# A pipelined cross-attention kernel: projections four tiles ahead of the scores in place of five

## The chip, the cores and the metric

The kernel runs on one core of a Trainium2 chip. The metric is the device time of one execution in microseconds (us); lower is better. Three runs of the kernel before took 222.98, 226.28 and 222.8 us, median 222.98. The core's compute engines are TensorE (PE), VectorE (DVE), ScalarE (ACT) and GpSimd (POOL); SyncE (SP) issues nearly all transfers. Each engine works through its own instructions in order, and they meet at semaphores.

## What is computed

Three residual blocks follow one another on 64 tokens of width 256: a cross attention to a context of 6272 rows, a self attention with 16 heads on dequantised weights, and a gated mixture of experts. The change touches the first, cut here to its core:

```python
q = x @ Wq.T;  k_raw = context @ Wk.T;  v_raw = context @ Wv.T     # 32 heads of 8
kv = concatenate([k_raw, v_raw], -1).reshape(b, m, 32, 8, 2);  k, v = kv[..., 0], kv[..., 1]
q = _rmsnorm(q);  k = _rmsnorm(k)              # over the 8 of a head
scores = einsum('bhnd,bhmd->bhnm', q, k) * 8 ** -0.5
out = einsum('bhnm,bhmd->bhnd', softmax(scores, -1), v)
x = x + out;  x = x + self_attention(layernorm(x));  x = x + experts(layernorm(x))
```

## The kernel before, in words

The context is cut into T = 49 tiles of 128 rows. Every engine walks the same sequence of steps t = FIRST .. LAST, written by `steps` (L94): warm-up steps with negative t, a hardware loop whose body holds eight steps, and closing steps. In one step an engine does its part for several tiles, each at its own distance from t. The constants of L55 are these distances: PROJ = 5, KV = 4, TR = 3, PV = -1. `step` of each engine asks for `t.ahead(distance)` and leaves the part out where that tile does not exist.

The way of tile k through a step pipeline:

- SP loads its context into `ctx_f` (four slots), `load`, L265.
- DVE rounds it to `ctx_hi` (`split_context`, L539, step k-PROJ-1) and POOL makes the rest `ctx_lo` (L351, same step). Both have two slots.
- PE projects keys and values into one of two PSUM banks: six matmuls of 512 columns, L809, L812 and L815, at the end of step k-PROJ.
- The keys' chain, step k-KV: ACT squares (`k_sq`, L421), DVE sums each head (`k_ss`, L557) and copies the values (L566), ACT takes logarithm and exponent (`k_ln` L431, `k_r` L435), DVE scales (`k_n`, L575) and writes the first two float16 parts of the keys (L583). For the first KV tiles (`HEAD = KV`) ACT copies the values, L424.
- POOL writes the third part (L357, semaphore `k2_done`), step k-TR.
- SP turns the keys with a DMA transpose, `k` to `kT`, both with four slots (`turn`, L272, L278). It waits for `k2_done` of its tile.
- PE multiplies queries and turned keys: the scores, two halves of eight matmuls, L773, step k. It waits for the turned keys (L767). ACT exponentiates each half (`exps`, L409) into `room`; the first half stands ahead of that step's `k_sq` in ACT's order, the second behind it.
- PE multiplies with the values one step later (L787).

So in PE's step t come the scores of tile t, the values of tile t-1, and the projection of tile t+PROJ.

SP's order is written apart from the steps: in `for t in range(2, T + LAG)` (L304, LAG = 7) it turns tile t-7, then loads context t, and on every third round issues codes (512 KB, one piece of the self attention's weights) or the scales for them. In this order: turn of a tile k that is a multiple of 3, load, codes; turn k+1, load, scales; turn k+2, load. The load waits for `ctx_lo` of tile t-4. POOL multiplies codes by scales (`dequantise`, L334, L343) at the end of its steps t = 3, 6, 9, ..., 48. The queries' own path (`queries_mm`, `queries_copied`, `queries_squared`, `queries_rms`, `queries_split`, `queries_turned`, `queries_placed`) is hung into the warm-up steps by the dictionaries at L437, L601 and L818.

In short, a "turn" below is one DMA transpose of SP, and S(k) is the moment at which the scores of tile k begin on PE.

Of the kernel before, what the change touches and what calls it, by code (L numbers as in the profile page):

```python
# [51 lines left out]
HC = H // 2  # L52
NR = E // 2 + 1
U = 8
PROJ, KV, TR, PV = 5, 4, 3, -1  # L55
FIRST, LAST = -(PROJ + 1), T - PV
HEAD = KV
LOOP0 = 1 - PV
# [35 lines left out]
def steps(engine, body, after):  # L94


    for c in range(FIRST, LOOP0):
        body(Tile(None, c))
        if c in after:
            after[c]()  # L100
    with engine.Fori(0, ITERS) as i:
        for j in range(U):
            body(Tile(i, LOOP0 + j))
    for c in range(LOOP1, LAST + 1):
        body(Tile(None, c))
# [8 lines left out]
def perceiver(nc, x, ctx_t, xwq, xwkv, codes, scales, wo_scales, qkv_bias, bo, gate_w, gate_bias,  # L114
              up_w, down_w, eye, expert_ids, pair_heads, out):
    with ExitStack() as stack:
# [256 lines left out]
        def _(act):  # L373
# [60 lines left out]
                    wait(act, kn_done, r.count(plus=-1))  # L434
                    nc.scalar.activation(k_r[:, a], k_ln[:, a], ACT.Exp, scale=-0.5).then_inc(r_done, 1)  # L435

            steps(act, step, {-4: queries_copied, -3: queries_rms})  # L437

            layernorm_act(act, "ln2")

# [54 lines left out]
        def _(dve):  # L495
# [102 lines left out]
                        values_copied(r)  # L598
                        keys_scaled(r)

            steps(dve, step, {-4: queries_squared, -3: queries_split, -2: queries_placed})  # L601


            dve.wait_ge(pv_done, 2 * T)
# [114 lines left out]
        def _(pe):  # L719
# [95 lines left out]
                        last = nc.tensor.matmul(ps_kv[a], ctx_lo[:, a, c], wkv_hi[:, c], start=False, stop=(c == DC - 1))  # L815
                    last.then_inc(kv_mm, 1)

            steps(pe, step, {-5: queries_mm, -2: queries_turned})  # L818

            pe.wait_ge(ready("o_sb"), 1)  # L820
            for h in range(2):
# [207 lines left out]
```

## Time and profile before

| | kernel before |
|---|---|
| median of three runs | 222.98 us |
| the profiled execution, its own time | 221.69 us |
| its span | 219.9 us |
| PE busy | 203.6 us, 93% |
| ACT busy | 147.5 us, 67% |
| DVE busy | 129.9 us, 59% |
| POOL busy | 106.8 us, 49% |
| granted TensorE clock, mean | 0.995 |
| transfers | 39.63 MB, mean 180 GB/s |

The profiled execution has its own time, 221.69 us, beside the median of the runs; its span, first to last instruction, is 1.8 us shorter. A PE busy for 93% need not be PE at its peak, and the share is an average over stages: the warm-up to 19.4 us, 49 tiles of cross attention to about 171 us, and then the self attention and the experts, which the change does not touch.

### The profile page before, as it was taken

The page shows a single profiled execution, that of the slowest core. Times are in us where ns is not written, and L with a number is a line of the kernel's source. Part 1 is how long each engine was busy: PE and PEld are TensorE (multiplying, and loading weights), DVE is VectorE, ACT ScalarE, POOL GpSimd, SP SyncE. Part 2 cuts the span into 40 slices and gives each one's busy share as a digit, 9 for nine tenths or more (in the row PEclk, how much of TensorE's full clock was granted, in tenths as well). Part 3 has the DMA queues.
Part 4 walks back from the last instruction along what each step waited for, and adds up shares of the span by engine and source line. Part 5 has one row for each costly group of instructions (what it writes and reads, how often), then busy time and mean ns, then how long its engine had stood idle before and what let it go on. Part 6 is the DMA issues. An engine that isn't in the chain of part 4 may idle for free.

```text
span 219.9 us, 7814 instructions
## 1 busy us (share of the span) xinstructions
PE 203.6 (93%) x2973; PEld 135.4 (62%) x2973; DVE 129.9 (59%) x325; ACT 147.5 (67%) x285; POOL 106.8 (49%) x125
## 2 busy tenths in 40 slices
PE   7676899999999999999999999999878889988993
PEld 2354577777777777777777777777656424463441
DVE  1688548666676776758676675776730522835721
ACT  3456788888888888888888888988789013313230
POOL 4335647748576665867658576665737000000000
PEclk9999999999999999999999999999999999999998
DMA  5429999999889998988979999999999997000000
GB/s 184 122 70 226 174 253 216 149 241 247 222 223 202 208 194 205 227 216 213 198 198 202 221 220 200 255 183 234 147 278 248 289 287 211 28 3 0 0 3 12
DMA packets 66816, 39.63 MB, mean 180 GB/s; under 512 B 54007, under 2 KB 60599, under 8 KB 66799
## 3 DMA queue, kind: packets, MB, share of 16 engines
q1 hardware_dynamic: 66367, 38.95, 79.1%
q10 hardware_dynamic: 432, 0.46, 0.7%
q8 instruction: 10, 0.16, 0.3%
q14 instruction: 7, 0.06, 0.1%
HBM read 26.49 MB, written 0.07 MB: 121 GB/s over the span
## 4 chain that ended last, share of the span: by engine, by line
PE 79%; DMA 7%; DVE 6%; ACT 3%; issue 2%; POOL 2%; ACTq 0%; DVEq 0%
PE ps L787 20%; PE ps L809 13%; PE ps L773 11%; PE ps L815 9%; PE ps L812 9%; PE ps L837 5%; DMA kT<-k 5%; PE ps L927 3%; DMA ctx_f<-ctx_t 2%; PE ps L943 2%; PE ps L888 2%; PE ps L846 1%; PE ps L876 1%; POOL k L357 1%; PE ps L935 1%
## 5 line engine op out<-in xcount | busy, mean ns | idle before, releaser
L409 ACT ACTIVATE room<-ps 128x1024 f32<-128x1024 f32 x98 | 100.2, 1029 | 21.1 <-PE ps L773 21.0
L351 POOL TENSOR_TENSOR ctx_lo<-ctx_f,ctx_hi 128x256 fp32r<-128x256 f32 x49 | 36.0, 734 | 54.6 <-DVE ctx_hi L551 52.2
L787 PE MATMUL ps<-room,v_flat 128*17 128x128 f32 x1568 | 52.3, 274 | 0.0
L809 PE MATMUL ps<-wkv_hi,ctx_hi 128*128 128x512 f32 x98 | 43.7, 446 | 2.6 <-DVE k_n L575 1.5
L787 PEld LDWEIGHTS ps<-room,v_flat 128*17 128x17 f32 x1568 | 38.6, 97 | 5.3 <-ACT room L409 0.3
L583 DVE CAST k<-k_n 128x512 f16<-128x512 f32 x49 | 37.9, 774 | 2.6
L812 PE MATMUL ps<-wkv_lo,ctx_hi 128*128 128x512 f32 x98 | 38.8, 396 | 0.4 <-DVE wkv_lo L502 0.4
L343 POOL TENSOR_TENSOR w_all<-w_all,s_ring 128x1024 f32<-128x1024 f32 x16 | 37.9, 2375 | 0.0
L575 DVE TENSOR_TENSOR k_n<-ps,k_r 128x256 f32<-128x256 f32 x49 | 20.8, 424 | 25.2 <-ACT k_r L435 25.2
L357 POOL TENSOR_TENSOR k<-k_n,k 128x256 f16<-128x256 f32 x49 | 33.1, 675 | 5.0 <-DVE k L583 5.0
L773 PEld LDWEIGHTS ps<-q_blk,kT 48*128 48x128 f16 x784 | 22.1, 94 | 21.7 <-issue 13.5
L773 PE MATMUL ps<-q_blk,kT 48*128 48x128 f16 x784 | 31.0, 218 | 3.5 <-DMA kT<-k 1.9
L557 DVE TENSOR_REDUCE k_ss<-k_sq 128x32 f32<-128x256 f32 x49 | 20.3, 415 | 21.9 <-ACT k_sq L421 21.9
L815 PE MATMUL ps<-wkv_hi,ctx_lo 128*128 128x512 f32 x98 | 30.8, 395 | 0.0
L809 PEld LDWEIGHTS ps<-wkv_hi,ctx_hi 128*128 128x128 f32 x98 | 18.4, 187 | 15.0 <-issue 8.6
L815 PEld LDWEIGHTS ps<-wkv_hi,ctx_lo 128*128 128x128 f32 x98 | 18.4, 188 | 4.3
L812 PEld LDWEIGHTS ps<-wkv_lo,ctx_hi 128*128 128x128 f32 x98 | 18.5, 189 | 2.8 <-DVE wkv_lo L502 0.7
L421 ACT ACTIVATE k_sq<-ps 128x256 f32<-128x256 f32 x49 | 18.5, 378 | 2.4 <-PE ps L815 2.4
L431 ACT ACTIVATE k_ln<-k_ss,eps_rms 128x32 f32<-128x32 f32 x49 | 16.1, 328 | 4.5 <-DVE k_ss L557 4.3
L566 DVE COPY v_flat<-ps 128x256 f32<-128x256 f32 x45 | 18.5, 412 | 0.0
L551 DVE CAST ctx_hi<-ctx_f 128x256 fp32r<-128x256 f32 x48 | 13.6, 283 | 0.1
L435 ACT ACTIVATE k_r<-k_ln 128x32 f32<-128x32 f32 x49 | 11.3, 230 | 1.6
(113 smaller groups left out, 123.0 us busy)
## 6 DMA issues: line engine op xcount, KB each, us to landing
w_all<-codes SPq DMA_DIRECT2D x16, 512.0 KB, 4.2
ctx_f<-ctx_t SPq DMA_DIRECT2D x48, 128.0 KB, 2.8
up_sb<-up_w SPq DMA_DIRECT2D x5, 704.0 KB, 10.1
s_ring<-scales SPq DMA_DIRECT2D x12, 256.0 KB, 3.8
s_ring<-wo_scales SPq DMA_DIRECT2D x4, 512.0 KB, 5.4
dn_sb<-down_w SPq DMA_DIRECT2D x5, 352.0 KB
kT<-k SPq DMA_TRANSPOSE x49, 3.7
wkv_f<-xwkv ACTq DMA_DIRECT2D x1, 256.0 KB, 3.2
```

What stands on the lines that cost most here:

```text
L343: nc.gpsimd.tensor_tensor(w, w, s, ALU.mult).then_inc(ring_free[u % RING], 1)
L351: nc.gpsimd.tensor_tensor(ctx_lo[:, split.slot(2)], ctx_f[:, split.slot(4)], ctx_hi[:, split.slot(2)].bitcast(F32), ALU.subtract).then_inc ...
L357: nc.gpsimd.tensor_tensor(key_part(keys, 2), k_n[:, keys.slot(2)].rearrange("p (r h d) -> p r h d", h=2, d=XD), key_part(keys, 0), ALU.sub ...
L409: nc.scalar.activation(probs[:, t.slot(2), half], ps_scores[half].rearrange("p b n -> p (b n)"), ACT.Exp).then_inc(exp_done, 1)
L557: nc.vector.tensor_reduce(k_ss[:, r.slot(2)], k_sq[:, r.slot(2)].rearrange("p (h d) -> p h d", d=XD), AX_X, ALU.add).then_inc(ss_done, 1)
L575: nc.vector.tensor_tensor(kn, ps_kv[r.slot(2)][:, 0:D].rearrange("p (h d) -> p h d", d=XD), k_r[:, r.slot(2)].unsqueeze(2).to_broadcast([P ...
L583: nc.vector.tensor_copy(key_parts(r)[:, :, :, 0:2, :], pairs.unsqueeze(3).to_broadcast([P, PAIRS, 2, 2, XD])).then_inc(k1_done, 1)
L773: last = nc.tensor.matmul(ps_scores[half][:, e, at:at + P], kT[rows, t.slot(4), r // 2], q_blk[rows, r // 2].rearrange("p h n -> p (h n)") ...
L787: last = nc.tensor.matmul(ps_o[CT * j:CT * j + VW, g * P:(g + 1) * P], v_sb[:, t.slot(8), r], probs[:, t.slot(2), half, at:at + P], start= ...
L809: nc.tensor.matmul(ps_kv[a], ctx_hi[:, a, c], wkv_hi[:, c], start=(c == 0), stop=False)
L812: nc.tensor.matmul(ps_kv[a], ctx_hi[:, a, c], wkv_lo[:, c], start=False, stop=False)
L815: last = nc.tensor.matmul(ps_kv[a], ctx_lo[:, a, c], wkv_hi[:, c], start=False, stop=(c == DC - 1))
```

## The change

The three distances ahead of the scores are each one smaller, the distance of the values stays, and the queries' steps move by one, so that they still stand behind the same projections. `FIRST`, `HEAD` and the loop's bounds follow from the constants.

```diff
-PROJ, KV, TR, PV = 5, 4, 3, -1
+PROJ, KV, TR, PV = 4, 3, 2, -1
...
-            steps(act, step, {-4: queries_copied, -3: queries_rms})
+            steps(act, step, {-3: queries_copied, -2: queries_rms})
...
-            steps(dve, step, {-4: queries_squared, -3: queries_split, -2: queries_placed})
+            steps(dve, step, {-3: queries_squared, -2: queries_split, -1: queries_placed})
...
-            steps(pe, step, {-5: queries_mm, -2: queries_turned})
+            steps(pe, step, {-4: queries_mm, -1: queries_turned})
```

On PE, at the end of the warm-up, this is the difference of the orders; L756 turns the queries, L773 is the first tile's scores, the rows of L809, L812 and L815 are one projection.

```order
 L815 MATMUL ps<-wkv_hi,ctx_lo 128x512 x2
 L756 MATMUL ps<-ident,q_room 128x64 x8
-L809 MATMUL ps<-wkv_hi,ctx_hi 128x512
-L812 MATMUL ps<-wkv_lo,ctx_hi 128x512
-L809 MATMUL ps<-wkv_hi,ctx_hi 128x512
-L812 MATMUL ps<-wkv_lo,ctx_hi 128x512
-L815 MATMUL ps<-wkv_hi,ctx_lo 128x512 x2
 L773 MATMUL ps<-q_blk,kT 128x128 x16
```

The projection of tile 4 no longer stands ahead of the scores of tile 0; it comes behind them, and every later projection stands behind one more tile's scores and values.

On ACT at the same place, L421 to L435 are the keys' chain and L409 is an exponent. Before:

```order
L421 ACTIVATE k_sq<-ps 128x256
L424 ACTIVATE v_flat<-ps 128x16x16
L431 ACTIVATE k_ln<-k_ss,eps_rms 128x32
L435 ACTIVATE k_r<-k_ln 128x32
L421 ACTIVATE k_sq<-ps 128x256
L424 ACTIVATE v_flat<-ps 128x16x16
L431 ACTIVATE k_ln<-k_ss,eps_rms 128x32
L435 ACTIVATE k_r<-k_ln 128x32
L409 ACTIVATE room<-ps 128x1024
L421 ACTIVATE k_sq<-ps 128x256
L409 ACTIVATE room<-ps 128x1024
```

The change:

```order
L421 ACTIVATE k_sq<-ps 128x256
L424 ACTIVATE v_flat<-ps 128x16x16
L431 ACTIVATE k_ln<-k_ss,eps_rms 128x32
L435 ACTIVATE k_r<-k_ln 128x32
L409 ACTIVATE room<-ps 128x1024
L421 ACTIVATE k_sq<-ps 128x256
L409 ACTIVATE room<-ps 128x1024
```

These are tiles 2, 3 and 4 before, and tiles 2 and 3 now: the chain of tile 3 has come behind the first exponent of tile 0.

On POOL, L351 makes `ctx_lo` and L357 the third part of the keys; the first dequantisation (L343) stands some rows below the piece.

```order
 L351 ISA
 L351 TENSOR_TENSOR ctx_lo<-ctx_f,ctx_hi 128x256 x4
-L357 TENSOR_TENSOR k<-k_n,k 128x16x2x8
-L351 TENSOR_TENSOR ctx_lo<-ctx_f,ctx_hi 128x256
 L357 TENSOR_TENSOR k<-k_n,k 128x16x2x8
 L351 TENSOR_TENSOR ctx_lo<-ctx_f,ctx_hi 128x256
```

One pair less stands ahead of each dequantisation. Before, the keys that come behind it are those of tiles 7, 10, 13, ...; now they are those of tiles 6, 9, 12, .... SP's order is the same in both kernels.

## Rows read from the trace of the kernel before

**Rows 1.** The table by stretches; columns named in its first row.

```profile
core 0: us, PE busy (x) PEld busy (x) DVE busy (x) ACT busy (x) POOL busy (x), PEclk, DMA share, GB/s
32.82:155.48 122.66, 122.66 (x2107) 89.18 (x2107) 84.04 (x195) 104.24 (x196) 83.79 (x92) 1.00 0.98 213
```

**Rows 2.** Timeline, PE: start us, us, operation; scores of tiles 1, 2, 4, 43, 44, 47.

```profile
22.43 0.62 PE L773 MATMUL ps<-q_blk,kT 48*128 48x128 f16 x16
...
26.53 0.62 PE L773 MATMUL ps<-q_blk,kT 48*128 48x128 f16 x16 [0.89 <-DMA kT<-k]
...
32.82 0.62 PE L773 MATMUL ps<-q_blk,kT 48*128 48x128 f16 x16
...
155.48 0.62 PE L773 MATMUL ps<-q_blk,kT 48*128 48x128 f16 x16
...
159.48 0.62 PE L773 MATMUL ps<-q_blk,kT 48*128 48x128 f16 x16 [0.79 <-DMA kT<-k]
...
166.11 0.62 PE L773 MATMUL ps<-q_blk,kT 48*128 48x128 f16 x16 [0.23 <-DMA kT<-k]
```

**Rows 3.** Timeline, all engines: the chain of tile 31, from S(27) to its turn.

```profile
105.16 0.62 PE L773 MATMUL ps<-q_blk,kT 48*128 48x128 f16 x16
...
106.60 0.38 ACT L421 ACTIVATE k_sq<-ps 128x256 f32<-128x256 f32 x1
...
107.82 2.37 POOL L343 TENSOR_TENSOR w_all<-w_all,s_ring 128x1024 f32<-128x1024 f32 x1
...
108.85 1.61 DVE L583 CAST k<-k_n 128x512 f16<-128x512 f32 x1
...
111.45 0.67 POOL L357 TENSOR_TENSOR k<-k_n,k 128x256 f16<-128x256 f32 x1
...
112.14 1.23 SPq L278 DMA_TRANSPOSE kT<-k  x1
```

**Rows 4.** Timeline, SP's queue: turns of tiles 30 and 32, codes, scales.

```profile
107.89 1.26 SPq L278 DMA_TRANSPOSE kT<-k  x1
...
109.82 0.42 SPq L281 DMA_DIRECT2D w_all<-codes  x1
...
114.05 0.57 SPq L287 DMA_DIRECT2D s_ring<-scales  x1
114.71 1.26 SPq L278 DMA_TRANSPOSE kT<-k  x1
```

**Rows 5.** L278 alone: issue to landing of the turns of tiles 30, 31, 32.

```profile
DMA to landing us min/median/max: 2.8/2.8/2.8
...
DMA to landing us min/median/max: 2.7/2.7/2.7
...
DMA to landing us min/median/max: 3.8/3.8/3.8
```

**Rows 6.** Timeline, SP's queue: first codes behind tile 3, turns of tiles 4, 5.

```profile
25.77 0.43 SPq L281 DMA_DIRECT2D w_all<-codes  x1
26.30 1.24 SPq L278 DMA_TRANSPOSE kT<-k  x1
...
28.88 1.62 SPq L278 DMA_TRANSPOSE kT<-k  x1
```

**Rows 7.** L278 alone: issue to landing of the turns of tiles 4 and 5.

```profile
DMA to landing us min/median/max: 5.1/5.1/5.1
...
DMA to landing us min/median/max: 6.9/6.9/6.9
```

**Rows 8.** L278 alone, by stretch: 50 to 132 us, 132 to 161 us.

```profile
DMA to landing us min/median/max: 2.7/3.2/4.4
...
DMA to landing us min/median/max: 3.1/4.7/7.7
```

**Rows 9.** The chain that ended last, in order of time: start us, us, what.

```profile
18.46 0.86 DVE q_blk L536 x2
...
160.29 5.77 DMA kT<-k
```

## The prediction

> **What bounds the kernel now.** I read first the table by stretches, then PE's timeline. Between S(4) and S(43) PE is busy for all of its 122.66 us, at a granted clock of 1.00 [rows 1]; the two starts lie 39 tiles apart [rows 2], so a step takes (155.48 - 32.82) / 39 = 3.145 us. ACT, the next engine, has 104.24 us of work there, 2.67 us a step, DVE and POOL 84 us, 2.15 us a step [rows 1]. So PE sets the step, and no other engine's amount of work is near it. Then I looked at what PE waits for outside this stretch. S(2), S(44) and S(47) each end a wait for turned keys, of 0.89, 0.79 and 0.23 us [rows 2]. The keys arrive just in time there. The question is how early they arrive in between.
>
> For that I followed one tile. Tile 31's chain begins on ACT behind the first exponent of step 27. S(27) is 105.16, its square starts at 106.60, the third part of the keys on POOL at 111.45, the turn is issued at 112.14 [rows 3] and lands 2.7 us later [rows 5], at 114.84. S(31) is 32.82 + 27 x 3.145 = 117.74. The keys lie ready for 2.9 us. The same for its neighbours: tile 30 is issued at 107.89 [rows 4] and lands 2.8 us later [rows 5], 3.9 us ahead of S(30) = 114.59; tile 32 is issued at 114.71 [rows 4], lands 3.8 us later [rows 5], 2.4 us ahead of S(32) = 120.88. This pattern of three comes from the weights: the dequantisation of 2.37 us [rows 3] stands ahead of tile 31's keys on POOL, and the scales are issued 0.66 us ahead of tile 32's turn [rows 4].
>
> **What the change does.** It adds no instruction and takes none away. The chain of a tile starts where it did relative to its projection, but the scores come one step, 3.145 us, sooner behind it. So each slack above shrinks by 3.145 us: 3.9 becomes +0.8, 2.9 becomes -0.2, 2.4 becomes -0.7. What had been cover is gone.
>
> PE is in order, so a wait for keys holds the next projection too, and with it the chain of a later tile. The first exponent of step t waits for the scores of t, and the square behind it on ACT is now that of tile t+3. So there is a closed loop: S(t) to landed keys of t+3 to S(t+3), with three steps, 9.44 us, to run in where there were four, 12.58. Where the loop takes longer, PE waits. The sum goes by stretches.
>
> *Middle, tiles 12 to 37.* The dequantisation moves to the tiles that are multiples of 3, and SP's order does not. Such a tile is turned S + 6.98 (112.14 - 105.16, [rows 3]), then come a load, the codes, and at once the next tile's turn. Codes follow a turn by 109.82 - 107.89 = 1.93 us [rows 4]. Today 2.3 us pass from codes to the next turn; with the late turn ahead of them about 0.5 us are left. One turn of today stands like that: tile 4's, 0.53 us behind its codes [rows 6]. It took 5.1 us [rows 7], landing 5.6 us behind the codes' issue. So the keys of tile 3n+1 land 6.98 + 1.93 + 5.3 to 5.6 = 14.2 to 14.5 us behind S(3n-3), and have four steps, 12.58 us. The excess of 1.6 to 1.9 us is met by two waits, three tiles apart, since the four steps hold a waiting step at either end: 0.8 to 0.95 us for each three tiles. If the codes delayed nothing, the multiples of 3 would still need 6.98 + 2.8 = 9.78 us, 0.34 over 9.44. Nine groups of three give 3.1 to 8.6 us. I take 0.8 each, 7.2 us, because the crowded turn is the nearer row.
>
> *Start, tiles 0 to 11.* Tile 4's projection no longer runs ahead of S(0), but S(0) waits for the placed queries, 18.46 plus 0.86 us [rows 9], as before: nothing gained. S(2) stays near 26.5. Tile 5's turn was issued 28.88 - 22.43 = 6.45 us after S(1) [rows 2, 6] and took 6.9 us [rows 7]. After S(2) the same chain ends at 26.53 + 6.45 + 6.9 = 39.9; S(5) was 35.97. That is +3.9 us, or +2.1 with tile 4's 5.1 us. The next tile of its kind, 8, may lose the lower of the two once more. Ends 2.1 and 6.0; I take 3.5, as a slower pace also unloads the queue.
>
> *Late, tiles 38 to 46.* The turns from 132 us on take 4.7 us in the median and up to 7.7, against 3.2 before that [rows 8]; now the scales are 512 KB each and stand ahead of the turns of tiles 38, 41, 44. Tile 32, of this kind, is turned S(28) + 6.4 (114.71 - 108.30, [rows 4]; S(28) from the step), so with 4.7 us tiles 38 and 41 need 11.1 us, 1.7 over 9.44 each. Tile 44 needed 159.4 - S(40) = 159.4 - 146.0 = 13.4 us, since S(44) waited for it [rows 2]: 4.0 over. Together 7.4; at least the 0.34 of above each, 1 us. I take 4 us, about half.
>
> *End.* S(44) to S(47) is 6.63 us [rows 2]. Tile 47's square now stands behind S(44), not S(43). From S(43) = 155.48 to its turn at 160.29 are 4.8 us [rows 2, 9], and the landing takes 5.8. So S(47) is 10.6 us behind S(44): +4.0 us; with a landing of 2.8 us +1.0. I take 2.5. One step less runs without a projection, where exponents bound; that gain (rival 3) is swallowed by this wait.
>
> Sum: 221.69 + 7.2 + 3.5 + 4 + 2.5 = 238.9 us for the profiled execution. The median of the runs stands 1.3 us above that execution, so 240 us. The ends of the four terms are 2.1 + 3.1 + 1 + 1 = 7 us and 26 us, that is 230 and 249.
>
> Beside this, the Trainium skill, "DMA: Bandwidth & Descriptors", Queues, rings and completion order, says that each engine consumes the descriptors of a ring in ring order, so what SP issues later waits behind its codes; the 5.1 us of a turn 0.53 us behind codes [rows 6, 7] agrees. The same page, Latency and other measured facts, says that lighter HBM load makes the fixed part of a transfer smaller; that speaks for rival 1.
>
> **Rivals.**
>
> 1. *The landings shrink.* With the DMA engines at 0.98 [rows 1], a slower pace may give the turns back their short landing, 2.8 us [rows 5], everywhere. For: the same instruction takes 2.7 to 7.7 us. Against: the crowding behind codes is a matter of order, and gets worse. Then the middle and late stretches cost 0.34 us per three tiles, 12 times, 4 us, the end 1 and the start 1: 228 to 230 us. Chance 0.2.
>
> 2. *Everything adds.* All recorded landings stay, and the late turns push one another: 6.0 + 8.6 + 7.4 + 4 = 26 us on top, 248 to 249 us and a little beyond, since a late tile can find its queue fuller still. Chance 0.13.
>
> 3. *No slower.* POOL and SP catch up because the chain, not PE, is what waits. What is left is the gain of one step less without a projection: such steps are bound by two exponents of about 1.0 us and PE's order around them, some 2.4 us against PE's 1.6, so 0.8 us. This needs every loop within 9.44 us, and decides at the point where tile 32's kind falls from 3.145 x 4 - 2.4 = 10.2 us by 0.7. For: nothing in the rows. 222 us. Chance 0.03.
>
> 4. *The clock falls.* The waits would take PE to its half clock; the other rivals are at 2.4 GHz, the granted 1.00. Against: the wait of 0.89 us ahead of S(2) [rows 2] left it there. If it happened for a tenth of the tiles, 5 tiles x 3 us, 15 more: 255 us. Chance 0.02.
>
> **How the numbers follow.** My forecast has 0.62, and its own range is 232 to 247. To hold 8 in 10, the range takes in most of rival 1 and reaches to the edge of rival 2: 229 to 249. A difference of 2%, 4.5 us, is about what a measurement of this kernel can tell from no change: slower by more means above 227.4. Only the lowest part of rival 1 and rival 3 lie below. Faster by over 2% has no source in the rows: 0.01. Within 2%: 0.05. Slower: 0.94.
>
> **What would show it.** In the changed kernel's trace PE waits for the turned keys, with L773 released by the DMA to `kT` or by the turn's issue, 10 to 17 us in all, where the trace of before has three, 1.9 us together [rows 2]. The step is 3.4 us on average, in a pattern of three: one wait of 0.8 us or more at tiles 3n+1, none or little at the others, and the turn of 3n+1 takes about 5 us with codes issued some 0.5 us ahead. ACT, DVE and POOL busy times stay as they are. From S(44) to S(47) more than 8 us pass. Self attention and experts take the same time as before. The prediction is wrong if the step stays below 3.2 us (then landings shrank), if the waiting tiles are of another kind (then I misjudged the loop), or if the start, to S(5), costs nothing.

## The result, and the profile after

| | before | changed |
|---|---|---|
| median | 222.89 us (4 runs) | 243.08 us (239.25 to 244.4, 4 runs) |
| ratio to before | | 1.083, 95% interval 1.063 to 1.104 |
| span of the profiled execution | 219.9 us | 241.0 us |
| PE busy | 203.6 us | 209.5 us, the same 2973 matmuls |
| granted TensorE clock, mean | 0.995 | 0.97 |

The change makes the kernel 8% slower. The ratio is taken over the runs outside the chip's slower state, 242.79 and 239.25 us for the changed kernel, so it is smaller than that of the medians. The forecast was 240 us, its range 229 to 249.

The table by stretches for the changed kernel, S(12) to S(37), where the kernel before needs 78.63 us:

```profile
core 0: us, PE busy (x) PEld busy (x) DVE busy (x) ACT busy (x) POOL busy (x), PEclk, DMA share, GB/s
62.49:151.87 89.38, 80.87 (x1351) 58.20 (x1351) 54.93 (x127) 66.37 (x126) 54.89 (x59) 0.98 0.82 189
```

PE is no longer busy throughout [rows 1]; 8.5 us are idle, and the rest is busy for longer at a clock of 0.98. No other engine has become the bound: ACT's share fell, and so did that of the DMA engines, from 0.98 to 0.82. What took over is latency. The waits of the changed kernel (engine, line waited for; us in total, times, longest us):

```profile
PE ps L773 <- DMA kT<-k: 17.0, 17, 3.1
PEld ps L773 <- DMA kT<-k: 6.4, 5, 3.4
```

The kernel before had three such waits of 1.9 us [rows 2]. (The weight loads of PE wait beside its matmuls; the two are not added.) The page's chain that ended last:

```profile
PE 38%; DMA 22%; issue 12%; ACT 8%; DVE 8%; POOL 6%; SPq 3%; ACTq 0%; DVEq 0%; POOLq 0%
```

Before, PE held 79% of that chain and DMA 7%. Now a turn of the keys stands in it, and ahead of it ACT, DVE and POOL, one after the other: the loop itself is the path. PE's timeline over two of its pieces, S(34) to S(41):

```profile
140.80 0.62 PE L773 MATMUL ps<-q_blk,kT 48*128 48x128 f16 x16
143.95 0.62 PE L773 MATMUL ps<-q_blk,kT 48*128 48x128 f16 x16
147.37 0.62 PE L773 MATMUL ps<-q_blk,kT 48*128 48x128 f16 x16 [0.21 <-DMA kT<-k]
151.87 0.62 PE L773 MATMUL ps<-q_blk,kT 48*128 48x128 f16 x16 [1.29 <-DMA kT<-k]
155.32 0.62 PE L773 MATMUL ps<-q_blk,kT 48*128 48x128 f16 x16 [0.23 <-DMA kT<-k]
158.47 0.62 PE L773 MATMUL ps<-q_blk,kT 48*128 48x128 f16 x16
161.61 0.62 PE L773 MATMUL ps<-q_blk,kT 48*128 48x128 f16 x16
165.39 0.62 PE L773 MATMUL ps<-q_blk,kT 48*128 48x128 f16 x16 [0.57 <-DMA kT<-k]
```

Steps without a wait are still 3.15 us. The long wait stands at tile 37, a tile 3n+1. SP's queue ahead of it, and the landing of that turn:

```profile
144.50 1.25 SPq L278 DMA_TRANSPOSE kT<-k  x1
...
146.42 0.42 SPq L281 DMA_DIRECT2D w_all<-codes  x1
146.94 1.23 SPq L278 DMA_TRANSPOSE kT<-k  x1
...
DMA to landing us min/median/max: 4.8/4.8/4.8
```

Tile 36, the multiple of 3, is turned 6.84 us after S(33) = 137.66; codes follow 1.92 us later; tile 37's turn is 0.52 us behind them and lands in 4.8 us, at 151.75, 5.3 us behind the codes. S(37) is 151.87. Before, the same kind of turn landed in 2.7 us [rows 3, 5].

By stretches, from the starts of the scores on PE in both traces (us; changed minus before is what the span lost):

| | before | changed | lost |
|---|---|---|---|
| start to S(0) | 19.41 | 20.46 | 1.05 |
| S(0) to S(12) | 38.57 | 42.03 | 3.5 |
| S(12) to S(37) | 78.63 | 89.38 | 10.75 |
| S(37) to S(44) | 22.87 | 23.80 | 0.9 |
| S(44) to S(48) | 8.24 | 12.83 | 4.6 |
| S(48) to the end | 52.2 | 52.5 | 0.3 |

The stretch from S(44) on holds one projection more than before: the step from S(44) to S(45) now projects tile 48 and takes 3.16 us, where it took 1.61.

### The profile page after: what moved, and what is told of

Same layout as the page of the kernel before. It is cut to its first block, busy times and chain, and to the rows that moved or that the text cites. A ratio compares the mean times of both kernels' runs of the same rounds, so it can differ in the third digit from the quotient of the medians.

```text
span 241.0 us, 7820 instructions
## 1 busy us (share of the span) xinstructions
PE 209.5 (87%) x2973; PEld 138.5 (57%) x2973; DVE 130.7 (54%) x326; ACT 146.9 (61%) x284; POOL 108.0 (45%) x125
## 4 chain that ended last, share of the span: by engine, by line
PE 38%; DMA 22%; issue 12%; ACT 8%; DVE 8%; POOL 6%; SPq 3%; ACTq 0%; DVEq 0%; POOLq 0%
DMA kT<-k 21%; PE ps L787 6%; PE ps L773 5%; PE ps L837 5%; PE ps L809 4%; PE ps L815 3%; POOL k L357 3%; PE ps L812 3%; ACT room L409 3%; POOL ctx_lo L351 3%; PE ps L927 3%; DVE k_n L575 2%; PE ps L943 2%; ACT k_sq L421 2%; ACT k_ln L431 2%
## 5 line engine op out<-in xcount | busy, mean ns | idle before, releaser
L409 ACT ACTIVATE room<-ps 128x1024 f32<-128x1024 f32 x98 | 100.5, 1029 | 43.4 <-PE ps L773 43.4
L351 POOL TENSOR_TENSOR ctx_lo<-ctx_f,ctx_hi 128x256 fp32r<-128x256 f32 x49 | 37.3, 761 | 71.5 <-DVE ctx_hi L551 69.9
L787 PE MATMUL ps<-room,v_flat 128*17 128x128 f32 x1568 | 53.6, 278 | 0.3 <-ACT room L409 0.3
L773 PE MATMUL ps<-q_blk,kT 48*128 48x128 f16 x784 | 31.7, 223 | 19.8 <-DMA kT<-k 17.0
L773 PEld LDWEIGHTS ps<-q_blk,kT 48*128 48x128 f16 x784 | 23.1, 97 | 39.1 <-issue 26.5
L809 PE MATMUL ps<-wkv_hi,ctx_hi 128*128 128x512 f32 x98 | 44.6, 455 | 0.7 <-DVE k_n L575 0.7
L787 PEld LDWEIGHTS ps<-room,v_flat 128*17 128x17 f32 x1568 | 39.1, 98 | 6.3 <-ACT room L409 0.7
L812 PE MATMUL ps<-wkv_lo,ctx_hi 128*128 128x512 f32 x98 | 39.6, 404 | 0.0
L343 POOL TENSOR_TENSOR w_all<-w_all,s_ring 128x1024 f32<-128x1024 f32 x16 | 37.8, 2363 | 1.2 <-DMA s_ring<-wo_scales 1.2
L583 DVE CAST k<-k_n 128x512 f16<-128x512 f32 x49 | 37.0, 755 | 2.1
L357 POOL TENSOR_TENSOR k<-k_n,k 128x256 f16<-128x256 f32 x49 | 33.1, 676 | 4.1 <-DVE k L583 4.1
L815 PE MATMUL ps<-wkv_hi,ctx_lo 128*128 128x512 f32 x98 | 32.3, 411 | 0.0
L809 PEld LDWEIGHTS ps<-wkv_hi,ctx_hi 128*128 128x128 f32 x98 | 18.6, 189 | 13.4 <-issue 9.0
L815 PEld LDWEIGHTS ps<-wkv_hi,ctx_lo 128*128 128x128 f32 x98 | 19.1, 196 | 4.8 <-POOL ctx_lo L351 0.3
L421 ACT ACTIVATE k_sq<-ps 128x256 f32<-128x256 f32 x49 | 18.5, 378 | 3.8 <-PE ps L815 3.8
L812 PEld LDWEIGHTS ps<-wkv_lo,ctx_hi 128*128 128x128 f32 x98 | 18.9, 193 | 2.5 <-DVE wkv_lo L502 0.2
L435 ACT ACTIVATE k_r<-k_ln 128x32 f32<-128x32 f32 x49 | 11.3, 230 | 1.6
```

Of the source, the lines that this page charges most:

```text
L343: nc.gpsimd.tensor_tensor(w, w, s, ALU.mult).then_inc(ring_free[u % RING], 1)
L351: nc.gpsimd.tensor_tensor(ctx_lo[:, split.slot(2)], ctx_f[:, split.slot(4)], ctx_hi[:, split.slot(2)].bitcast(F32), ALU.subtract).then_inc ...
L357: nc.gpsimd.tensor_tensor(key_part(keys, 2), k_n[:, keys.slot(2)].rearrange("p (r h d) -> p r h d", h=2, d=XD), key_part(keys, 0), ALU.sub ...
L409: nc.scalar.activation(probs[:, t.slot(2), half], ps_scores[half].rearrange("p b n -> p (b n)"), ACT.Exp).then_inc(exp_done, 1)
L421: nc.scalar.activation(k_sq[:, a], ps_kv[a][:, 0:D], ACT.Square).then_inc(sq_done, 1)
L583: nc.vector.tensor_copy(key_parts(r)[:, :, :, 0:2, :], pairs.unsqueeze(3).to_broadcast([P, PAIRS, 2, 2, XD])).then_inc(k1_done, 1)
```

## The experiments

Theory: the distance sets a loop, S(t) to landed keys of t+3, that has three steps to run in, and its longest member, a turn crowded behind 512 KB of codes, decides. Rivals: the shorter distance costs whatever stands in the queues; the landings are set by the load of the DMA engines and not by order; the clock.

Each run below is the changed kernel with one edit, except where said. "Middle" is S(12) to S(37) in its trace: 78.6 us before, 89.4 us changed. The kernel before had a median of 222.80 us beside four of the runs (TR = 3 alone, little traffic, hardly any dequantisation, dequantisation one step later) and 222.75 us beside the other four.

### A shorter chain: the third part of the keys one step earlier

```diff
-PROJ, KV, TR, PV = 4, 3, 2, -1
+PROJ, KV, TR, PV = 4, 3, 3, -1
```

> The changed kernel with one number different: TR = 3, so POOL makes the third part of the keys one step earlier in its own order, ahead of the next tile's ctx_lo instead of behind it, and the turn can be issued about 1 us earlier (near S + 4.9 us in place of 5.7 to 7.0). Theory (a loop of three steps, S to landed keys, is too long by 0.3 to 1.9 us): every loop now fits in 9.44 us, PE no longer waits in the middle, 221 to 226 us. Rival (the turns' landing behind codes and scales is what costs, whenever they are issued): the waits stay, 233 us or more.

Measured: 239.44 us (238.46 to 239.99), ratio 1.078 (1.071 to 1.085). The middle takes 86.75 us. The number is the rival's; my theory had overlooked something. Most turns do go out 4.8 to 5.0 us after their S, 0.9 us sooner. But tile 37's, 0.52 us behind the codes again, lands in 4.9 us, and the start grows too: S(0) to S(12) takes 44.4 us, 42.03 in the changed kernel. POOL and SP show why:

```profile
140.43 2.44 POOL L343 TENSOR_TENSOR w_all<-w_all,s_ring 128x1024 f32<-128x1024 f32 x1
142.83 0.91 POOL L351 TENSOR_TENSOR ctx_lo<-ctx_f,ctx_hi 128x256 fp32r<-128x256 f32 x1
```

```profile
143.81 0.34 SPq L270 DMA_DIRECT2D ctx_f<-ctx_t  x1
144.20 0.42 SPq L281 DMA_DIRECT2D w_all<-codes  x1
144.72 1.24 SPq L278 DMA_TRANSPOSE kT<-k  x1
```

The load that follows the turn of 3n waits for a `ctx_lo` that stands behind the dequantisation on POOL, as it did before the edit. What the edit moved is the turn: its keys now stand ahead of the dequantisation, so the turn goes out early and the load has to wait. SP is in order, so the codes wait with it and leave just ahead of the next turn. The next run takes this one wait away.

### The same, with the load's wait moved one tile back

```diff
-PROJ, KV, TR, PV = 4, 3, 2, -1
+PROJ, KV, TR, PV = 4, 3, 3, -1
...
-LAG = 7
+LAG = 6
```

With LAG = 6 the load behind the turn of tile k is that of tile k+6 in place of k+7, and waits for the `ctx_lo` of tile k+2 in place of k+3.

> The changed kernel with TR = 3 and LAG = 6. TR = 3 alone left a wait at tiles 3n+1: SP's load behind the turn of 3n waits for a ctx_lo that then stands behind the dequantisation, so load and codes went out 0.5 us ahead of the next turn. With LAG = 6 that load waits for a ctx_lo made before, codes go out 2 us behind the turn of 3n, and 2.3 us stay ahead of the turn of 3n+1. Theory (loop length, with crowding by order as its largest piece): every loop is at most 9.5 us (5.9 + 2.8, 5.3 + 4.2), PE waits in hardly any step of the middle, 221 to 227 us. Rival (three steps of distance are too few whatever stands in the queues, or the load of DMA itself makes the landings): 234 us or more.

Measured: 228.98 us (227.6 to 230.88), against 222.75 us for the kernel before beside it, ratio 1.027 (1.021 to 1.033). That is 2 us above my expectation, and 10.5 us less than the run above, for one load's place. In the two traces 7.8 us of it come in the middle and 5.6 us from S(0) to S(12); S(0) itself is 1.9 us later. SP's queue for the same tiles, and the landing of tile 37's turn:

```profile
130.49 1.25 SPq L278 DMA_TRANSPOSE kT<-k  x1
131.83 0.53 SPq L270 DMA_DIRECT2D ctx_f<-ctx_t  x1
132.41 0.42 SPq L281 DMA_DIRECT2D w_all<-codes  x1
134.45 1.23 SPq L278 DMA_TRANSPOSE kT<-k  x1
...
DMA to landing us min/median/max: 2.9/2.9/2.9
```

2.04 us instead of 0.52 lie between codes and turn, and the turn lands in 2.9 us; over the middle such turns, 1.7 to 2.0 us behind the codes, take 2.9 to 3.8 us. The middle is PE's own again:

```profile
59.34:138.25 78.91, 78.75 (x1352) 57.13 (x1352) 51.80 (x125) 66.30 (x126) 54.71 (x59) 1.00 0.95 209
```

So three steps of distance are enough in the middle, at a DMA share of 0.95, with little to spare: the keys of tiles 28, 29 and 32 land 0.15 us or less ahead of their scores. The crowding of the middle came from the order in SP's queue, not from the load of the DMA engines, which is higher here than in the changed kernel. LAG = 6 without TR = 3 was not run. What is left over the kernel before lies in the start (S(12) is 1.4 us later), at the late tiles 38 and 43 (2.1 us together; tile 38's turn stands 0.69 us behind 512 KB of scales, tile 43's 1.98 us behind codes), and at the end: S(44) to S(48) takes 12.57 us against 8.24.

### Little traffic from codes and scales

The loads of codes and scales bring 64 columns; POOL fills the whole unit from the scales.

```diff
-                sp.dma_start(w_all[:, u], codes[:, u]).then_inc(codes_in[u % RING], 16)
+                sp.dma_start(w_all[:, u, 0:64], codes[:, u, 0:64]).then_inc(codes_in[u % RING], 16)
...
+                w = w_all[:, u].rearrange("p (c n) -> p c n", n=64)
+                s = s_ring[:, u % RING, 0:64].unsqueeze(1).to_broadcast([P, WS // 64, 64])
-                nc.gpsimd.tensor_tensor(w, w, s, ALU.mult).then_inc(ring_free[u % RING], 1)
+                nc.gpsimd.tensor_tensor(w, s, s, ALU.mult).then_inc(ring_free[u % RING], 1)
```

> The changed kernel with codes and scales loaded for 64 columns alone, one eighth to one sixteenth of the bytes; POOL multiplies broadcast scales over the whole unit, so its time stays and the self attention's weights are not the real ones. Theory (ring order behind 512 KB): all turns land in 2.7 to 3 us, the wait at 3n+1 goes, what is left is 6.98 + 2.8 = 9.8 us for the multiples of 3, 0.34 us per three tiles: 224 to 229 us. Rival (the latency is in the engines' chain): 236 us or more.

Measured: 230.38 us (229.62 to 231.13), ratio 1.037 (1.030 to 1.045). Landings and the middle; below them the changed kernel's landings from 62 to 129 us:

```profile
DMA to landing us min/median/max: 2.7/2.7/3.0
...
61.44:140.22 78.78, 78.70 (x1352) 57.13 (x1352) 50.41 (x125) 66.29 (x126) 49.57 (x59) 1.00 0.58 132
```

```profile
DMA to landing us min/median/max: 2.7/3.5/5.6
```

The chain on the engines is as in the changed kernel, and PE does not wait: the loss of the middle is in the landings. Even the 0.34 us per three tiles that I had left for the multiples of 3 is gone; they are turned 6.1 to 6.7 us after their S in place of 6.6 to 7.0, and fit but for one wait of 0.15 us. The total is 1.4 us above the expected interval: in the trace S(0) to S(12) still loses 3.0 us against the kernel before, S(44) to S(48) takes 12.5 us and loses 4.3, and 1.7 us are lost behind S(48).

Codes and scales are hardly the cause of the first two: beside the same small loads the turns of the middle land in 2.7 to 3.0 us, and yet six turns of this trace take 4.2 to 5.2 us, those of tiles 4, 7, 9, 43, 46 and 48; every other from tile 1 on takes at most 3.1. From the DMA queues (packets, MB, share) while tile 48's turn is under way, and that turn's landing; below them the one queue that is used from 75 to 149 us, where no turn takes over 2.9 us:

```profile
q8 instruction: 1, 0.02, 1.7%
...
kT<-k SPq DMA_TRANSPOSE x1, 4.5
```

```profile
q1 hardware_dynamic: 30532, 9.77, 58.2%
```

Each of the six turns has one packet of 16 KB on q8 under way, of the kind that the profile calls `instruction`, for 0.9 to 1.3 us, which ends 2.6 to 3.2 us behind the turn's issue; the turn lands 1.2 to 2.0 us behind that packet's end. No other turn of the trace has such a packet later than 0.7 us behind its issue, and from 51 to 157 us there is none. (Packets of 8 KB of the same kind, on q14 at 64, 74 and 149 us, stand beside turns of 2.7 to 2.8 us.) So a turn can be late beside a load of program code as well as behind codes. That is read off the trace and was not tested by an edit.

### Hardly any dequantisation

POOL multiplies 8 columns of each row by their scales and leaves the others as they were loaded; all loads stay.

```diff
-                nc.gpsimd.tensor_tensor(w, w, s, ALU.mult).then_inc(ring_free[u % RING], 1)
+                part = (slice(None), slice(None), slice(0, 8)) if u < NQKV else (slice(None), slice(0, 8))
+                nc.gpsimd.tensor_tensor(w[part], w[part], s[part], ALU.mult).then_inc(ring_free[u % RING], 1)
```

> The changed kernel with dequantisation on 8 columns per row in place of 512 or 1024, so that it takes far less than 2.37 us on POOL (the self attention's weights are not the real ones); all loads stay. Theory: the multiples of 3 are turned 1.1 us sooner, at S + 5.75, codes leave sooner, and keys 3n+1 land S(3n-3) + 5.75 + 1.93 + 5.4 = 13.1 against 12.6: about 0.25 us per three tiles instead of 0.8 to 1, and the start and the late stretch gain alike: 227 to 233 us. Rival (transfers alone decide): 238 us or more.

Measured: 235.78 us (232.44 to 239.19), too spread for an interval, and between my two numbers. The middle takes 82.35 us, 3.7 over the kernel before, where I expected about 2. The multiples of 3 are turned 5.7 to 6.1 us after their S, the turns of 3n+1 land in 2.7 to 4.7 us. So the dequantisation has a part in the loss by what it does to SP's timing, as the theory says, but less clearly than the transfers.

### Dequantisation one step later

```diff
-DEQ0, DEQ = 3, 3
+DEQ0, DEQ = 4, 3
```

> The changed kernel with dequantisation at POOL's steps 4, 7, 10 in place of 3, 6, 9, which puts it ahead of the keys of tiles 3n+1 again, as in the kernel before, with 2.3 us between codes and that turn. Theory: the crowded turn of 3n+1 (5 us) goes away and the waits of 1.4 us at tiles 3n+1 with it; the next longest loop is that of tiles 3n+2 with 6.3 + 3.9 = 10.2 us, so PE waits there, up to 0.76 us per three tiles: 232 to 238 us. Rival (only the alignment of dequantisation and codes costs, not the shorter distance): within 2 us of the kernel before, 225 us.

Measured: 241.09 us (239.25 to 242.43), ratio 1.088 (1.081 to 1.096): no gain that the intervals separate, 3 us above my expectation. The middle is 83.68 us, 5.7 us better than the changed kernel, and the waits are where I expected them: 0.7 to 0.9 us at tiles 3n+2 (20, 26, 32), about 0.2 at 3n+1. The late tiles lost part of what the middle had won: S(37) to S(44) takes 26.2 us against 23.8, with waits of 1.6, 1.5 and 0.9 us at tiles 38, 43 and 44. The turns of 38 and 44 stand 0.7 and 1.5 us behind scales of 512 KB. In these traces the alignment moves the loss more than it removes it.

### One distance less again

`PROJ, KV, TR = 3, 2, 1`, the queries' steps packed into steps -3 to -1.

```diff
-PROJ, KV, TR, PV = 4, 3, 2, -1
+PROJ, KV, TR, PV = 3, 2, 1, -1
...
-LOOP0 = 1 - PV
+LOOP0 = 3 - PV
```

> Distances one smaller again: PROJ, KV, TR = 3, 2, 1, the queries' steps packed into the warm-up steps -3 to -1. Theory (the step is the loop from S to landed keys over PROJ - 1 steps): loops of 8.5 to 9.8 us over two steps, 4.2 to 4.9 us a step in place of 3.4, that is 280 to 305 us. Rival (each distance less costs a fixed wait as this change did, 18 to 21 us): 258 to 266 us.

Measured: 289.5 us, one run.

```profile
73.68:182.34 108.66, 80.41 (x1351) 57.25 (x1352) 45.60 (x126) 66.28 (x125) 55.13 (x59) 1.00 0.60 154
```

A step is 108.66 / 25 = 4.35 us, so a loop of two steps is 8.7 us, 5.7 to 6 us to the turn and 2.8 for the landing: the queue is slack (share 0.60) and the bare loop is what is seen. A loop of 8.7 us fits into three steps of PE, 9.44, and not into two, 6.29. One run of 289.5 us is far outside the rival's 258 to 266.

### The clock over the first scores

```diff
                 last.then_inc(ready("qT_mm"), 1)
+                for _ in range(11):
+                    nc.tensor.matmul(ps[:, 7, :], zeros[:, 0:P], zeros[:], start=True, stop=True, skip_group_check=True)
```

> The changed kernel with eleven extra matmuls on zeros (128 x 512, float16, about 2.4 us) behind the turned queries, into a free PSUM bank, where PE waits 2.6 us for the placed queries. Theory: the granted clock stays up over the first scores, tile 4's projection takes 1.6 instead of 2.3 us, S(1) and S(2) come up to 1 us sooner, and the middle does not change: 0 to 2 us less than the changed kernel. Rival (the clock is no part of the loss): the projection takes 2.3 us as before.

In the changed kernel PE waits 2.62 us for the placed queries, where the kernel before projects tile 4, and works at half clock after it (L815 takes 1.05 in place of 0.63 us):

```profile
20.46 0.62 PE L773 MATMUL ps<-q_blk,kT 48*128 48x128 f16 x16 [2.62 <-DVE q_blk L536]
...
22.36 1.05 PE L815 MATMUL ps<-wkv_hi,ctx_lo 128*128 128x512 f32 x2
```

With the filler, in the trace of its slowest run (248.82 us):

```profile
18.26 2.55 PE L760 MATMUL ps<-zeros 128*128 128x512 f16 x11
20.95 0.62 PE L775 MATMUL ps<-q_blk,kT 48*128 48x128 f16 x16
...
22.53 0.63 PE L817 MATMUL ps<-wkv_hi,ctx_lo 128*128 128x512 f32 x2
24.06 0.62 PE L775 MATMUL ps<-q_blk,kT 48*128 48x128 f16 x16 [0.90 <-DMA kT<-k]
```

The projection runs at full clock, and a wait of 0.90 us for tile 1's keys spends what it wins. S(2) still comes 0.55 us sooner behind S(0) than in the changed kernel; at S(4), which waits 2.6 us for keys, nothing is left (15.2 us from S(0), 14.2 in the changed kernel). Measured: 244.61 us (242.96 to 248.82), ratio 1.096 (1.088 to 1.103): no gain. The clock does fall at this place in the changed kernel, and keeping it up here brought nothing that the runs can tell; the falls elsewhere were not tested.

### The two numbers of TR = 3 and LAG = 6 on the kernel before

TR is one more and LAG one less here too.

```diff
-PROJ, KV, TR, PV = 5, 4, 3, -1
+PROJ, KV, TR, PV = 5, 4, 4, -1
...
-LAG = 7
+LAG = 6
```

> The kernel before, distances 5, 4 and the keys' third part and SP's order as in the run above: TR = 4, LAG = 6. Theory: the step is PE's own 3.145 us already, so 1 us more slack for each tile gains nothing in the middle, and only the three waits of 1.9 us at tiles 2, 44 and 47 can go: 219 to 223 us. Rival (waits hidden in the rows cost PE time in the middle of the kernel before): 217 us or less.

Measured: 220.74 us (219.77 to 222.98, 12 runs) against 222.75 us (17 runs), ratio 0.9913 (0.9876 to 0.9949): 0.9% faster, small but clear of 1, and the fastest of the versions here. The middle is 78.6 us as before, S(2) and S(44) wait for no keys, one wait of 0.55 us is left at S(47), and the keys lie ready 2.8 to 4.9 us ahead of the scores in the middle. Its S(0) was at 20.74 in this trace, 1.3 us later than in the kernel before, and S(2) was at 26.53 all the same. The spans differ by only 0.6 us in the two profiled executions; that the other 1.4 us of the medians come from such late starts, which more slack absorbs, is a guess that no run here tests.

## Why the prediction was right or wrong

- **What bounds, and what takes over**: right. PE's 3.145 us a step stayed where no wait stood, and PE came to wait for turned keys, 17.0 us in 17 waits, at the top of the 10 to 17 us given.
- **Middle, 7.2 us forecast, 10.75 measured.** From S(19) to S(37) 5.3 us are lost in 18 tiles, 0.88 us for each three; the sum had 0.8, its reason 0.8 to 0.95. The parts of the loop measured 6.84 + 1.92 + 5.3 us at tile 37, forecast 6.98 + 1.93 + 5.3 to 5.6. I spread the excess over two waits, and it came as one of about 1.3 to 1.5 us at every second tile 3n+1 (19, 25, 31, 37) with 0.2 to 0.3 us around it. The mis-sized term is tiles 12 to 19, with 5.5 us lost: tile 13 alone waited 2.14 us, its turn taking 5.6 us and landing 6.4 us behind the codes where the sum had at most 5.6; and behind that wait came the clock.
- **The clock**, rival 4 with 0.02: it happened, in small. Behind the wait at tile 13 the projection's first matmul takes 0.79 us for 0.50, and the next step is 4.41 us long:

```profile
67.85 0.62 PE L773 MATMUL ps<-q_blk,kT 48*128 48x128 f16 x16 [2.14 <-DMA kT<-k]
68.40 1.07 PE L787 MATMUL ps<-room,v_flat 128*17 128x128 f32 x32
69.40 0.79 PE L809 MATMUL ps<-wkv_hi,ctx_hi 128*128 128x512 f32 x1
```

  That is 1.3 us, and 0.3 in the step after it, of half clock (1.2 GHz); the waits of 1.3 us at tiles 19 to 37 left it up. Over the whole kernel PE is busy 5.9 us longer for the same matmuls. The prediction had argued from one wait of 0.89 us; the late and closing terms of my own sum held waits of more than 2 us. How much of the 5.9 us lies on the path is not settled; near S(0) the filler gained nothing.
- **Start, 3.5 us forecast, 1.05 + 3.5 measured.** Size about right, place half wrong: tile 5 waits for nothing, its turn landing in 4.1 us and not 6.9; tiles 4 (1.1 us), 7 (2.2) and 10 (0.5) wait, which are 3n+1 as in the middle. But the crowding of the middle does not explain them: the codes were issued 1.0 to 2.3 us ahead, not 0.5, and with little traffic the same stretch still loses 3.0 us. The turns of tiles 4 and 7 have an `instruction` packet under way and land 1.6 and 1.2 us behind its end. So had the rows that the term went by: the 6.9 us of tile 5 [rows 7] end 1.1 us behind such a packet. That S(0) gains nothing was right. It lost 1.05 us; the trace shows half clock at 10 us (L736 takes 1.82 us, 1.08 before), a place that the change does not touch.
- **Late, 4 us forecast, 0.9 measured**: wrong in size. I carried tile 44's 7.7 us over, half; the turn took 4.5 us at the slower pace, and the kernel before had already paid 0.85 us there, which the 4.0 us of the sum counts again. The 7.7 us had an `instruction` packet in them, and ended 1.1 us behind it.
- **End, 2.5 us forecast, 3.4 to S(47), 4.6 to S(48)**: the mechanism holds, the value was taken too low between its ends of 1.0 and 4.0. The landing of tile 47 did not shorten (5.2 us). Ahead of it S(46) waits 3.1 us, the longest wait of the kernel, for a turn 0.67 us behind 512 KB of codes and beside an `instruction` packet, 6.2 us long; the sum had no such term. The changed kernel and the five above with PROJ = 4 and no filler take 12.5 to 12.8 us from S(44) to S(48), even with little traffic. A part of that belongs to the distance itself: steps without a projection are shorter, and three of them are shorter than the loop. An estimate from the run with little traffic: turns go out 4.8 us after S(43) to S(45) and could land in 2.75 us, a loop of 7.6 us, so S(48) would be 3.15 + 7.6 = 10.8 us behind S(44), 2.5 more than before. The other 1.8 of that run's 4.3 us is the landing of tile 48's turn, 4.5 us beside an `instruction` packet.
- **Rivals.** "The landings shrink", in the middle: wrong for the crowded turns (tiles 13, 19, 25, 31 and 37, 4.8 to 5.6 us at a DMA share of 0.82), right for the multiples of 3 (2.7 to 2.8 us, 2.8 to 3.6 before), and not clear for tiles 3n+2 (2.7 to 4.7 us, 3.6 to 4.4 before). "No slower" needed every loop within 9.44 us; the run with TR = 3 and LAG = 6 comes to that in the middle, and still ends 2.7% slower. Its gain of 0.8 us has the wrong sign: since S(0) gains nothing, the projection that left the warm-up is one more behind S(0), and the step from S(44) to S(45) takes 3.16 us for 1.61. The errors of the terms, 3.6 us too little for the middle, 1.0 for the start, 2.1 for the end, 0.3 behind it and 3.1 too much for the late tiles, leave 3.9 of 21.1 us: the total is closer than its parts, and that is in part luck.
- The Trainium skill, "DMA: Bandwidth & Descriptors", Queues, rings and completion order, which the prediction had set beside the price of the crowding, says that each DMA engine consumes descriptors in ring order. The runs agree: tile 37's turn 0.52 us behind the codes took 4.8 us, 2.04 us behind them 2.9.

## What to carry to other kernels

A look-ahead in a pipeline is a loop: work out the time from the consumer's start to the landed data of the tile ahead, and compare it with the number of steps times the step; below that it costs nothing, above it each step pays. In that loop count what is queued ahead of the small, urgent transfer, because a large one issued just before it cost 2 us, and moving one load's wait, with TR = 3, was worth 10 us. Judge the opening and the closing steps apart: the closing ones are shorter, so the same distance buys less time, and in both the small transfers can meet loads of program code, which the profile lists under a queue of their own.

## What the runs showed of the hardware that I had not expected

- A turn of the keys takes 2.7 us from issue to landing with no codes or scales issued in the 5 us before it (the multiples of 3). In the middle of the changed kernel it took 4.8 to 5.6 us when issued 0.5 to 0.7 us behind 512 KB, at a DMA share of 0.82; it landed 5.3 to 6.4 us behind the issue of the large transfer (tiles 37 and 13).
- With little traffic from codes and scales, a turn with a 16 KB `instruction` packet under way took 4.2 to 5.2 us, six of six, and landed 1.2 to 2.0 us behind the packet's end. The two go together; that the one causes the other was not tested.
- Waits of 1.3 to 1.5 us (tiles 19, 25, 31, 37) left TensorE at 2.4 GHz, and so did 1.7 and 1.9 us in the run with TR = 3 (tiles 13 and 25, steps of 3.14 and 3.15 us behind them). One of 2.14 us (tile 13) and one of 2.62 us (S(0)) were followed by 1.2 GHz, and one of 2.12 us at tile 7 was not: the step behind it took 3.14 us.
- DVE's total changes with what POOL does beside it: the cast of L583 takes 0.43 us in the median and 1.61 us beside a dequantisation [rows 3]. With hardly any dequantisation it takes at most 0.82 us, and DVE is busy for 115.8 us in place of 130.7.
